# Who issues the first loads: context and Wk from ScalarE's queue instead of SyncE's

## What is computed

```
x = x + attn(layernorm(x), ctx; Wq, bq, Wk, bk, Wv, bv, Wo, bo)      # 16 heads of 32
x = x + (gelu((layernorm(x) @ U1) @ V1 + b1) @ U2) @ V2 + b2
# attn: q = a @ Wq + bq; k = ctx @ Wk + bk; v = ctx @ Wv + bv
#       softmax(clip(q k' * 32**-0.5)) v @ Wo + bo
```

## Time and profile before

| | us |
|---|---|
| median of 3 runs | 552.60 (552.56 to 552.63) |
| the profiled execution, its own time | 552.76 |
| its span, first to last instruction | 551.0 |
| PE busy | 543.4 (99%) |
| DVE, ACT, POOL busy | 466.8, 312.7, 371.7 |

### The profile page before, as it was taken

How to read it: one execution, slowest core, us unless ns; L and a number is a source line. 1 busy time by engine, 2 the same in 40 slices (tenths; PEclk the granted TensorE clock), 3 DMA queues, 4 the chain that set the end, 5 groups by cost and what they waited for, 6 DMA issues and landing times.

```text
span 551.0 us, 12063 instructions
## 1 busy us (share of the span) xinstructions
PE 543.4 (99%) x4818; PEld 463.0 (84%) x4818; DVE 466.8 (85%) x694; ACT 312.7 (57%) x524; POOL 371.7 (67%) x295
## 2 busy tenths in 40 slices
PE   8999999999999999999999999999999999999997
PEld 8998889888988898889887788888888888888885
DVE  5798999888988898889989778989899897978694
ACT  4565455545554555455465656757575757666663
POOL 1688677778877887787696556757474756665581
PEclk9999999999999999999999999999999999999999
DMA  8422362332233123351313130130311222101012
GB/s 320 176 82 97 108 237 78 98 116 63 74 96 116 59 79 98 115 195 56 134 44 109 62 115 1 39 115 19 88 66 63 72 78 77 59 19 58 20 58 95
DMA packets 25695, 50.36 MB, mean 91 GB/s; under 512 B 2984, under 2 KB 3368, under 8 KB 25256
## 3 DMA queue, kind: packets, MB, share of 16 engines
q1 hardware_dynamic: 25352, 49.07, 25.9%
q10 hardware_dynamic: 288, 0.52, 0.3%
HBM read 32.49 MB, written 16.78 MB: 89 GB/s over the span
## 4 chain that ended last, share of the span: by engine, by line
PE 88%; POOL 4%; DVE 3%; issue 1%; ACT 1%; DMA 0%; DVEq 0%; POOLq 0%; ACTq 0%
PE bank L1111 52%; PE ps_s L1111 16%; PE bank L1193 5%; PE ps_s L1163 5%; PE bank L1209 4%; PE bank L1240 2%; PE bank L1132 2%; POOL ss L435 2%; POOL ss L443 1%; POOL xs L456 1%; DVE ssum L883 1%; ACT ss L644 1%; PE bank L1258 1%; PE ps_s L1284 1%; DVE ss L869 1%
## 5 line engine op out<-in xcount | busy, mean ns | idle before, releaser
L565 POOL TENSOR_TENSOR hs_r<-ss,hs_r 128x512 fp32r<-128x512 f32 x63 | 88.9, 1411 | 90.8 <-ACT hs_r L793 90.8
L708 ACT ACTIVATE ss<-ps_s,once 128x512 f32<-128x512 f32 x128 | 88.0, 689 | 64.7 <-PE ps_s L1111 61.1
L1111 PE MATMUL ps_s<-p1t_r,v_r 128*128 128x512 f32 x384 | 111.1, 398 | 0.0
L1111 PE MATMUL bank<-hs_r,u_r 128*128 128x512 f32 x381 | 107.4, 391 | 0.0
L435 POOL TENSOR_TENSOR ss<-ss,smax 128x1232 f32<-128x1232 f32 x32 | 72.3, 2260 | 45.8 <-DVE smax L878 45.8
L1111 PE MATMUL bank<-wqo_r,ot_r 128*128 128x512 f32 x384 | 95.0, 396 | 0.0
L1111 PEld LDWEIGHTS bank<-hs_r,u_r 128*128 128x128 f32 x381 | 71.3, 188 | 16.0 <-DVE hs_r L938 0.5
L1111 PEld LDWEIGHTS bank<-wqo_r,ot_r 128*128 128x128 f32 x384 | 69.8, 188 | 14.1 <-issue 0.2
L1111 PEld LDWEIGHTS ps_s<-p1t_r,v_r 128*128 128x128 f32 x384 | 69.8, 188 | 13.5 <-issue 0.4
L443 POOL TENSOR_TENSOR ss<-ss,rsum 128x1024 f32<-128x1024 f32 x32 | 63.8, 1995 | 16.7 <-DVE rsum L885 16.7
L638 ACT ACTIVATE pt<-bank 128x512 f32<-128x512 f32 (+1 forms) x96 | 47.1, 527 | 43.5 <-PE bank L1193 43.0
(11 more groups left out here) (101 smaller groups left out, 895.7 us busy)
## 6 DMA issues: line engine op xcount, KB each, us to landing
xs<-in_x SPq DMA_DIRECT2D x64, 256.0 KB, 3.5
y_between<-xs SPq DMA_DIRECT2D x32, 256.0 KB, 2.0
fw<-y_between SPq DMA_DIRECT2D x4, 1024.0 KB, 5.5
xs<-y_between SPq DMA_DIRECT2D x4, 1024.0 KB, 5.4
out<-fw SPq DMA_DIRECT2D x16, 256.0 KB, 2.0
out<-xs SPq DMA_DIRECT2D x15, 256.0 KB, 2.0
xs<-in_Wo SPq DMA_DIRECT2D x1, 1024.0 KB, 8.5
fw<-in_v SPq DMA_DIRECT2D x1, 1024.0 KB, 5.2
```

The source lines that it names most:

```text
L565: pool.tensor_tensor(hs[:, c % 4, 1, :], hg[:, c % 4, :], hs[:, c % 4, 0, :].bitcast(F32), ALU.subtract)\
L708: act.activation(hg[:, c % 4, :], ps_s[:, c % 4, :], ACT.Gelu_apprx_tanh, bias=b1_c[:, c:c + 1]).then_inc(h_gelu, 1)
L1111: mm = pe.matmul(ps, lhs(a), rhs(c), start=first and i == 0, stop=last and i == len(PASSES) - 1)
```

## The change

ACT issues the load of the context and the two loads of Wk, as the first three instructions of its program; SP no longer has them, and goes from the two row tiles of block 0 straight on to the pieces of Wq. Transfers, sizes, destinations and semaphores are the same.

```
             load_x(0, 0)
-            sp.dma_start(once[:, UB * D - KC * B * KV:], ctx_bias).then_inc(in_ctx, 16)
-            for half in range(2):
-                sp.dma_start(wk_f[:, half, :, :], wk[half]).then_inc(in_wk[half], 16)
             for i, rows in enumerate(QROWS):
                 sp.dma_start(wq_f[0][:, rows, :], wq[0][:, rows, :]).then_inc(in_wq_rows[i], 16)
...
+            act.dma_start(once[:, UB * D - KC * B * KV:], ctx_bias).then_inc(in_ctx, 16)
+            for half in range(2):
+                act.dma_start(wk_f[:, half, :, :], wk[half]).then_inc(in_wk[half], 16)
 
             turned_z(0, 0)
```

## The result

| | before | changed |
|---|---|---|
| median, us | 552.61 (10 runs, 552.51 to 552.93) | 553.87 (10 runs, 553.65 to 555.58) |
| profiled execution, its own time | 552.76 | 555.46 |
| span | 551.0 | 553.7 |

The change makes the kernel slower by 1.26 us: ratio 1.0027, 95% interval 1.0018 to 1.0035 (the ratio of the medians alone is 1.0023; two late runs raise the other). Two of the ten runs stand apart, at 555.46 and 555.58, with a mean granted clock of 0.997 instead of 1.000; the other eight lie between 553.65 and 554.00. The profile is one of the two, so it holds two effects that have to be read apart.

The account below looks back on a forecast made before the run. PE was taken as the bound, its start hanging on z from x's two row tiles. Terms 0 + 0 + 1.6 + 0 on the profiled 552.76 gave 554.36, or 554.2 us as a median (+0.29%), range 552.5 to 555.0.

Parts of the forecast that it names:

- What bounds the opening: PE's start at 6.88 us hangs on z, from x's two row tiles; context, Wk and Wq are not late.
- The transfers of two queues at once: Opening loads: context and Wk beside x delay tile 1's statistics; +1.6 us taken, between +0.6 and +1.8.
- the even turns: Opening loads: queues alternate packet for packet, so tile 1 is through after 1.17 MB, at 5.6 us; +1.8 us.
- my 0.43 from bytes to landing: Row tile 1 of x: 0.43 us between its bytes being through, about 3.6, and its landing at 4.03.
- Whole transfers take turns: Rival, opening loads: with x first, tile 1 lands at 4.9 us; +0.6 us, 553.2; chance 0.22.
- ACT's transfers fall in behind x: Rival, opening loads: ACT's three come behind both x tiles, tile 1 lands at 4.03; 552.6 us; chance 0.12.
- The row of bv: bv, issued by ACT at 10.5 us, had no q10 packet in 10.6 to 13.5 while q1 moved 1.27 MB.
- SP's early Wq: 0: SP's queue: Wq's first piece issued 1.42 us earlier gains nothing, as PE has no wait for it; 0.
- The table load: 0: ACT's opening: table load ends at 3.42 us, covered before the copy at 7.58 with 4.2 us to spare; 0.
- The shift goes to the end whole: PE's work from 6.88 us runs without a gap, so the +1.6 us reaches the kernel's end whole.
- The clock: Rival, PE's wait for z: clock falls to half level in a 2.5 us gap; +3.0 us, 555.6; chance 0.10.
- The range: Whole kernel: 552.5 to 555.0 us, from the no-change case, leaving out the clock's case and the unseen one.

Follow-up runs that it names:

- the one-queue kernel: Kernel before, all on SP's queue, row tile 1 issued behind the context and Wk's first half; 556.92 us, ratio 1.0080.
- all five executions with these loads: Profiled executions of the changed kernel and four experiments issuing the same loads in the same order; second statistics at 5.54, 5.29, 5.42, 5.67 and 5.97 us.
- this run: Changed kernel with ACT's three issues held until the identity matrix is ready at 1.53 us; 554.14 us, ratio 1.0029.
- the test: Kernel before, with ACT waiting for row tile 1, then issuing bv ahead of its table load; 553.53 us, ratio 1.0018.

## Why the prediction was right

*What bounds the opening.* Right. PE's start hangs on the two tiles of x, and in the changed kernel the chain leads through tile 1.

*The transfers of two queues at once: the term that was mis-sized.* I had the mechanism, and the value +1.6 between bounds of +0.6 and +1.8; it measured +1.25 in the profiled execution (+1.0 to +1.7 in five), and 554.2 became 553.87. The first step that was off is the rates, which I took from one execution. In the changed kernel the engines moved more:

```profile
1.60:2.50 0.90, 0.90 (x5) 0.90 (x6) 0.00 (x0) 0.37 (x1) 0.40 (x1) 1.00 0.80 229
2.50:3.60 1.10, 1.10 (x7) 1.10 (x7) 0.00 (x0) 0.91 (x1) 0.00 (x0) 1.00 1.01 367
3.60:4.90 1.30, 1.30 (x8) 1.30 (x7) 0.87 (x3) 0.00 (x0) 0.00 (x0) 1.00 0.90 349
4.90:6.00 1.10, 1.10 (x12) 1.05 (x10) 0.47 (x1) 0.00 (x0) 0.00 (x0) 1.00 1.02 358
```

That is 0.21 + 0.40 + 0.45 = 1.06 MB by 4.9 us, where I had 0.90. The number of queues isn't the cause, since the one-queue kernel, with the same bytes ahead of tile 1, moved 1.04 MB by then. The first stretch varies most from one execution to the next. Here is one queue with 14 transposes, then two queues with the K product first:

```profile
1.60:2.50 0.90, 0.90 (x5) 0.90 (x6) 0.00 (x0) 0.41 (x1) 0.41 (x1) 1.00 0.78 205
...
1.60:2.50 0.90, 0.90 (x5) 0.90 (x6) 0.00 (x0) 0.37 (x1) 0.40 (x1) 1.00 0.55 77
```

The second step is that the turns were even only after the first stretch. The queues of the changed kernel in 1.5 to 2.2 us, then in 3.5 to 4.9 us:

```profile
q1 hardware_dynamic: 42, 0.09, 45.4%
q10 hardware_dynamic: 9, 0.02, 12.4%
...
q10 hardware_dynamic: 102, 0.30, 54.2%
q1 hardware_dynamic: 105, 0.19, 36.6%
```

x had a start of 42 packets to 9, then 105 to 102. That start is there in all five executions with these loads: from 1.6 to 2.5 us SP's queue is ahead of ACT's by 20 to 44 packets. With the rates measured here, the even turns' 1.17 MB would have been through at 4.9 + 0.11/0.358 = 5.2 us instead of my 5.6, and with my 0.43 from bytes to landing tile 1 would be there at 5.64; it landed at 5.51. The last 0.13 may be the head start, but one execution can't show so little, and the 0.43 itself was 0.8 in the run with one queue.

*Whole transfers take turns.* Out as the whole account: x would have landed at 4.9, not 5.51, and the earliest of the five executions has its statistics at 5.29. But the value lies between the two rules, and one window can't say how many packets a turn has.

*ACT's transfers fall in behind x.* Out at level starts, and yet the mechanism is real: 0.8 us later on the same queue it is what happens (3 packets to 259). The row of bv and this run agree that what has been handed over goes first, whichever queue brings it. I gave it 0.12 and a turning point of "bytes after about 3.0 us"; the run has it with an issue at 1.57.

*SP's early Wq: 0.* Right in the changed kernel, where PE waits for neither Wk nor Wq. It isn't free in general: with ACT's issues held back, it cost 1.0 of the 1.25 us that x had won back.

*The table load: 0.* Right; ACT was idle for 5.89 us ahead of its first copy, and in the test the load ran later still without harm.

*The shift goes to the end whole.* Right. Second statistics against time, each from one profiled execution with the clock up: 4.75 and 553.03, 5.09 and 553.27, 5.67 and 553.99, 6.00 and 554.31. From 4.29 that is 0.46, 0.80, 1.38 and 1.71 later, for 0.43, 0.67, 1.39 and 1.71 over the median of 552.6. So close a match is partly luck: the execution with 4.29 itself took 552.76.

*The clock.* Real: 2 of 10 runs, which doesn't contradict my 1 in 10. The price of 1.4 (13 matmuls in 3.0 us, against the same 13 at the pace of 14 in 1.8, give 1.33) measured 1.64, and the K product's matmuls showed it as 452 ns, not the 424 of a transpose. My ground for thinking it unlikely was wrong: at the kernel's end it held for 3.2 us behind PE's last matmul, but that is one case and no guarantee. In the changed kernel's profile PE's `keep_warm` ended at about 6.2 (1.59 + 4.60), PE was back at work at 8.16, and the clock was down from about 8.2: 0.61 in 8 to 9 us is 0.2 us at 1.00 and the rest at 0.50.

*The range.* 552.5 to 555.0 began at no change and ended ahead of the two late runs, so it would have held a gain of nothing too. What bears the prediction out is less the range than the chain, which leads through tile 1.

## What to carry to other kernels

A second queue adds little capacity when the engines are already at a share of 1 (1.06 MB by 4.9 us with two, 1.04 with one): whatever it starts earlier, it takes from the transfer that is first needed. Find the one load on which the chain hangs and let nothing be handed over before or beside it; even a transfer that is "only" moved forward, on the same queue or another, has to be priced by what it stands ahead of. And a wait of TensorE (2.0 us here) costs more than its length when the clock falls behind it (1.64 us more), so a profile of one execution should be held against the times of all runs before it is believed.

## What the runs showed of the hardware that I had not expected

- The rate of the first transfers is a matter of the execution more than of the queues. In 1.6 to 2.5 us it was 112, 118, 118 and 205 GB/s in four kernels with one queue, and 77 to 229 in eight with two. From 2.5 to 3.6 us it was 314 to 402 with one and 337 to 380 with two.
- A landing read from one execution is uncertain by some tenths of a us: 4.03 and 4.80 for tile 1 with the same transfers ahead of it, and statistics from 5.29 to 5.97 in the five executions with the changed loads.
- A head start of some 0.4 us at the issue decided who went first across queues: SP's queue, with x, 259 packets and ACT's, with the context, 3, in 1.9 us. Level issues gave even turns, 105 to 102, in 3.5 to 4.9 us.
- The granted clock fell some 2.0 us behind the end of PE's work in the profiled execution, and the mean clock says so of a second of the ten runs. With 14 instead of 26 transposes at the start it had not risen by 12 us. Ten executions with 26 transposes took 4.44 to 5.71 us for them, since the clock rose at a different time in each.
- A printed clock of 1.00 isn't proof of the full level: it stands beside matmuls of 462 instead of 294 ns with 14 transposes, and beside the 424 ns of the first transposes. The durations have to be read with it.
